# A graph network's second sum: rows sorted by source in three parts instead of one

## The reference

```
h = max(layernorm(x), 0)
msg = h[src] @ W_msg.T + b_msg + edge_embed[type]
x = x + gru(segment_sum(msg, dst), h)
h = max(layernorm(x), 0)
agg = segment_sum(h[dst], src)
z = ((1 + eps) * h + agg) @ W1.T + b1
x = x + relu(batchnorm(z) * gamma + beta) @ W2.T + b2
```

## Time and profile before

| | us |
|---|---|
| median of 3 runs | 6133.05 |
| lowest and highest | 6127.13 and 6144.72 |
| the profiled execution | 6150.87 |
| its span, first to last instruction | 6148.8 |
| busy in the span: PE, PEld | 3286.6, 2671.0 |
| DVE, ACT, POOL | 2171.7, 2000.3, 3592.3 |
| mean granted TensorE clock | 0.642 |

### The profile page before, as it was taken

How to read it: one execution, slowest core, us unless ns; L and a number is a source line. 1 busy time by engine, 2 the same in 40 slices (tenths; PEclk the granted TensorE clock), 3 DMA queues, 4 the chain that set the end, 5 groups by cost and what they waited for, 6 DMA issues and landing times.

```text
span 6148.8 us, 85445 instructions
## 1 busy us (share of the span) xinstructions
PE 3286.6 (53%) x19136; PEld 2671.0 (43%) x19137; DVE 2171.7 (35%) x4141; ACT 2000.3 (33%) x4208; POOL 3592.3 (58%) x3971
## 2 busy tenths in 40 slices
PE   4555556666666666667733333333433333337776
PEld 4444445445544544546532333222323323237775
DVE  8444444444444444445600000000000000027774
ACT  5222222222222222223522222221222212238886
POOL 2555556566665665663266666666666666666651
PEclk8555556665666556658755555555555555569999
DMA  4222211111111111111222222222212222236664
GB/s 141 57 58 56 55 52 42 41 42 42 43 43 40 43 43 40 43 43 53 65 72 71 73 71 71 72 71 69 74 68 75 71 69 74 69 114 224 221 221 142
DMA packets 251756, 466.50 MB, mean 76 GB/s; under 512 B 66550, under 2 KB 169129, under 8 KB 237581
## 3 DMA queue, kind: packets, MB, share of 16 engines
q0 software_dynamic: 106944, 226.05, 12.4%
q1 hardware_dynamic: 144717, 239.48, 11.9%
HBM read 315.00 MB, written 150.28 MB: 76 GB/s over the span
## 4 chain that ended last, share of the span: by engine, by line
another core or an unknown queue 34%; issue 24%; PE 23%; ACT 7%; SPq 6%; DVE 3%; ACTq 1%; DMA 1%; POOL 1%; DVEq 0%; POOLq 0%
PE ps L1563 7%; PE ps L1535 6%; PE ps L1410 4%; PE ps L1424 3%; ACT sb_counts L702 2%; SPq L405 2%; ACT ps L709 2%; SPq L406 2%; SPq L407 1%; PE ps L1432 1%; ACT sb_ring L788 1%; ACTq L784 1%; SPq L416 1%; DVE sb_oh L1237 1%
## 5 line engine op out<-in xcount | busy, mean ns | idle before, releaser
L573 POOL DMA_INDIRECT sb_ring<-msg_table,sb_idxslot x1664 | 1581.1, 950 | 1098.0 <-SPq L418 619.5
L603 POOL DMA_INDIRECT rows_by_src<-sb_ring,sb_idxslot x1664 | 1617.0, 972 | 864.4 <-issue 503.3
L1535 PE MATMUL ps<-sb_H,sb_oh 128*128 x3520 | 865.5, 414 | 1540.9 <-issue 1130.9
L1535 PEld LDWEIGHTS ps<-sb_H,sb_oh 128*128 128x128 f32 x3520 | 724.8, 299 | 1681.7 <-issue 1678.7
L1410 PE MATMUL ps<-sb_ring,sb_oh 128*128 x3520 | 849.2, 415 | 328.6 <-SPq L414 172.7
L1237 DVE TENSOR_SCALAR sb_oh<-sb_oh,sb_cf 128x512 f32<-128x512 bf16 x440 | 206.4, 492 | 2188.2 <-remote 1425.1
L1410 PEld LDWEIGHTS ps<-sb_ring,sb_oh 128*128 128x128 f32 x3520 | 734.7, 305 | 398.9 <-issue 392.2
L702 ACT CAST sb_counts<-ps 54x512 bf16<-54x512 f32 x440 | 254.4, 578 | 1919.0 <-remote 1030.5
L788 ACT COPY sb_ring<-ps 128x512 f32<-128x512 f32 x416 | 242.1, 582 | 1791.8 <-remote 1290.9
L1123 DVE TENSOR_TENSOR sb_Y<-sb_Y,ps 128x512 f32 x440 | 300.6, 683 | 746.8 <-remote 485.9
L1563 PE MATMUL ps<-sb_oh,sb_H 128*128 128x128 f32 x3520 | 432.6, 281 | 163.0 <-issue 116.8
(11 more groups left out here) (216 smaller groups left out, 3571.6 us busy)
## 6 DMA issues: line engine op xcount, KB each, us to landing
sb_H<-rows_by_src SPq DMA_DIRECT2D x110, 1088.0 KB, 5.0
sb_oh<-step_targets SPq DMA_DIRECT2D x110, 512.0 KB
sb_ring<-msg_table,sb_idxslot POOLq DMA_INDIRECT x1664
rows_by_src<-sb_ring,sb_idxslot POOLq DMA_INDIRECT x1664
rows_by_src<-sb_cf SPq DMA_DIRECT2D x198, 68.0 KB
msg_table<-sb_oh SPq DMA_DIRECT2D x14, 448.0 KB, 3.2
sb_oh<-in_x SPq DMA_DIRECT2D x49, 128.0 KB, 2.1
x_after_layer<-sb_H SPq DMA_DIRECT2D x49, 128.0 KB, 1.9
```

The source lines that it names most:

```text
L573: pool.indirect_dma_start(out=ring[:, r * G + q, 0:F], out_offset=None, in_=table_d[:, :], in_offset=bass.IndirectOffsetOnAxis(ap=idxslot[ ...
L603: pool.indirect_dma_start(out=rows_d[:, :], out_offset=bass.IndirectOffsetOnAxis(ap=idxslot[:, h, g * G + q:g * G + q + 1], axis=0), in_=r ...
L1535: m = mm(picked_ps[:, ds(slot, P)], pick[g][:, q * P:(q + 1) * P], H[:, ds(off, P)], start=False, stop=True, skip_group_check=True)
```

## The change

The tiles are cut into three parts of 768, 512 and 384 tiles (PASSES). Within each part the edges are sorted by source on their own: each part has its own starts of the 98 blocks (base_s has three rows), its own pads after each block, and its own stretch of rows_by_src: 55, 39 and 31 chunks, 125 in all (ALLC) against 110. As soon as all scatters of a part have landed, its chunks are summed within the pick stage (overlapped_sum on PE, sum_keys and sum_add on DVE, srows_in on SP), with two chunks of rows in flight; PICK_PHASES says in which pairs: none up to pair 27, then four sum chunks in each of the pairs 28 to 40 and three in 41, none in 42 and 43, four in each of 44 to 52 and three in 53. That is 94 chunks (OV). The last 31 are summed afterwards as before, with their counts set on by OV.

In the overlapped sums DVE alone makes the one-hots of the keys (four steps at a time) and adds the banks. ACT zeroes nothing: PE writes zeros to columns 128 to 511 of the bank with one matmul, and the group's first matmul begins its 128 columns anew (start).

In layer 0 DVE adds up the four one-hots of a group into one (block_sums, blks), so that rank_before and rank_after are one matmul each and not four. Where a part begins, PE sets the rank bank to that part's base (fresh).

In the prologue the digit one-hots are made from the packed edges in the tiles' own order, read back from DRAM (digit_fields at the third norm turn), so that each part is counted for itself; two of the 13 pieces follow after the loop. Pads: two for each block of each part, 588 in all against 196, each with one register load instead of two, over the first 294 groups of layer 0; the unused ends of the three stretches are filled with four larger pad blocks at the start. The table of the sums' blocks (sum_blocks) is worked out in the tail of layer 0 and not at its start.

```diff
+PASSES = (768, 512, 384)
+USED = [n + BLOCKS for n in PASSES[:-1]] + [(PASSES[-1] * P - PADS) // P + BLOCKS]
+SCHUNKS = [-(-(n + BLOCKS) // CH) for n in PASSES]
+FIRST_C = [sum(SCHUNKS[:z]) for z in range(NPASS)]
+OV = FIRST_C[-1]
+FCH = SCHUNKS[-1]
+ALLC = OV + FCH
...
         def rank_before(slot):
-            for q in range(G):
-                m = nc.tensor.matmul(rank_ps, before_b[:, :], own_blocks(slot)[:, q, :], start=False, stop=True,
-                                     skip_group_check=True)
-            return m
+            return nc.tensor.matmul(rank_ps, before_b[:, :], blks[:, slot, :], start=False, stop=True, skip_group_check=True)
...
+        def pick_loop(engine, body):
+            for a, b, s0, n in PICK_PHASES:
+                def pair(j):
+                    for k in range(2):
+                        sums = [((j - a) * 4 + s0 + i, (s0 + i) % 2) for i in range(2 * k, min(2 * k + 2, n))] if n else []
+                        body(j, k, sums, s0 if j is a and k == 0 and s0 in FIRST_C else None)
...
+            def pad_tile(a, b):
+                t = sp.value_load(lastrow[:, a, ds(b, 1)], min_val=0, max_val=ROWS_D - CH * P + CH - 1)
+                sp.dma_start(rows_d[ds(t, P, CH), :], const("pad")).then_inc(S("pads_out"), 16)
...
-            with sp.Fori(1, BLOCKS // RGROUPS) as j:
+            with sp.Fori(1, padded // RGROUPS) as j:
                 for r in range(RGROUPS):
                     relay(j, r)
                     pad_tiles(j * RGROUPS + r)
...
+            def landed(z):
+                for r in range(RGROUPS):
+                    sp.wait_ge(S(f"ring_dma{r}"), GATHERED + TILES_BY[z] // (RGROUPS * G) * G * 16)
+
+            def feed(j, k, sums, first):
+                c = j * 2 + k
+                if first is not None:
+                    z = FIRST_C.index(first)
+                    landed(z)
+                    for s, h in ((first, first % 2), (first + 1, 1 - first % 2)):
+                        wait(sp, "sum_done", (s - 1) * GPC)
+                        srows_in(s, h)
+                if not (isinstance(c, int) and c + 2 >= CHUNKS):
+                    sp.wait_ge(S("pick_oh"), (c + 1) * GPC)
+                    loc_in(c + 2, k)
+                for s, h in sums:
...
+                        sp.wait_ge(S("sum_done"), (s + 1) * GPC)
+                        srows_in(s + 2, h)
...
+            def block_sums(n, slot):
+                dve.wait_ge(S("blk_made"), n + 1)
+                vs.tensor_reduce(blks[:, slot, :], own_blocks(slot).rearrange("p q b -> p b q"), axis=AX.X, op=ALU.add) \
+                    .then_inc(S("blk_ready"), 1)
...
                         dve.wait_ge(S("rank_read"), n + 1)
                         vs.tensor_reduce(posE[:, ds(n * G, G)], own_ranks, axis=AX.X, op=ALU.add)
+                        block_sums(n + 1, (g + 1) % G)
...
+            def sum_keys(s, k, g):
+                if g == 0:
+                    dve.wait_ge(S(f"rows_in{k}"), rows_turn(s, k))
+                wait(dve, "sum_done", (s - 1) * GPC + g + 1)
+                vs.tensor_tensor(skeys[g].rearrange("p (q e) -> p q e", e=P),
+                                 srows[k][:, g * G:(g + 1) * G, KEY:KEY + 1].to_broadcast([P, G, P]),
+                                 iota_f.unsqueeze(1).to_broadcast([P, G, P]), ALU.is_equal).then_inc(S("key_oh_v"), 1)
+
+            def sum_add(s, g, offs):
+                n = s * GPC + g
+                dve.wait_ge(S("sum_done"), n + 1)
+                wait(dve, "bank_free", n)
+                yb = Y[:, ds(offs[g], 512)]
+                vs.tensor_tensor(yb, yb, bank(GPC + g), ALU.add).then_inc(S("bank_free"), 1)
+
+            def picks_and_sums(j, k, sums, first):
+                offs = [group_offsets(s, sumrow, (regs, regs_o)[i]) for i, (s, h) in enumerate(sums)]
+                layer1_pick(j, k)
+                for i, (s, h) in enumerate(sums):
+                    for g in range(GPC):
+                        sum_keys(s, h, g)
+                        if i:
+                            sum_add(sums[0][0], g, offs[0])
+                for g in range(GPC if sums else 0):
+                    sum_add(sums[-1][0], g, offs[-1])
...
+            def overlapped_sum(s, h):
+                step_offsets(s, sumrow)
+                for g in range(GPC):
+                    pe.wait_ge(S("key_oh_v"), s * GPC + g + 1)
+                    wait(pe, "bank_free", (s - 1) * GPC + g + 1)
+                    mm(bank(GPC + g)[:, P:], zeros_b[:, 0:P], zeros_b[:, P:], start=True, stop=True)
+                    for q in range(G):
+                        o = bank(GPC + g)[:, 0:P] if q == 0 else ps[:, GPC + g, ds(rel(g, q), P)]
+                        m = mm(o, srows[h][:, g * G + q, 0:F], skeys[g][:, q * P:(q + 1) * P],
+                               start=q == 0, stop=True, skip_group_check=True)
+                    m.then_inc(S("sum_done"), 1)
+
+            def picks_and_sums(j, k, sums, first):
+                picks(j, k)
+                for s, h in sums:
+                    overlapped_sum(s, h)
```

More of the change, by code:

```diff
@@ L63 @@
 DROWS, DW = DCOLS * NHI, DCOLS * NLO
+DIG_AT = 3
 NG = 2
@@ L235, in build_gnn @@
         lastf = small(BLOCKS)
-        lasti = [small(BLOCKS, i32) for _ in range(2)]
         possl = small(G, i32)
@@ L481, in _ @@
             loc_in(1, 1)
-            with sp.Fori(1, PAIRS) as j:
-                for k in range(2):
-                    sp.wait_ge(S("pick_oh"), (j * 2 + k - 1) * GPC)
-                    loc_in(j * 2 + k, k)
+            def feed(j, k, sums, first):
[10 more added lines that the diff above has]
+                for s, h in sums:
+                    after = [FIRST_C[z + 1] for z in range(NPASS - 1) if isinstance(s, int) and s < FIRST_C[z + 1]]
+                    if not (isinstance(s, int) and s + 2 >= after[0]):
+                        sp.wait_ge(S("sum_done"), (s + 1) * GPC)
+                        srows_in(s + 2, h)
@@ L608, in scatter @@
                         place_idx(b + 1, 1 - h, posE)
-            pool.wait_ge(S("pads_out"), (2 * BLOCKS + 2) * 16)
+            pool.wait_ge(S("pads_out"), 16 * sum(SCHUNKS[z] - USED[z] // CH for z in range(NPASS)) + NPASS * BLOCKS * 32)
             pool.wait_ge(S("posE_ready"), 1)
@@ L1447, in layer0 @@
                             rank_after((g + 3) % G).then_inc(S("rank_counted"), 1)
+                        if fresh is not None and g == 0:
+                            mm(rank_ps, ident, base_s[:, fresh, :], start=True, stop=True)
                         pe.wait_ge(S("blk_ready"), n + 1)
@@ L1457, in _ @@
             pe.wait_ge(S("base_s"), 1)
[L1458 to L1463 removed]
+            for z in range(NPASS):
+                a, b = (TILES_BY[z] - PASSES[z]) // (2 * CH), TILES_BY[z] // (2 * CH)
+                layer0(a, 0, fresh=z)
+                layer0(a, 1)
+                with pe.Fori(a + 1, b) as j:
+                    for k in range(2):
+                        layer0(j, k)
             for c in range(TCHUNKS, CHUNKS):
@@ L1617, in shape_constants @@
     put("blk", np.arange(NBK))
-    put("step", np.arange(SB) * P + np.arange(P)[:, None])
+    steps = np.arange(SS) * P + np.arange(P)[:, None]
+    put("step", steps)
+    put("done", -(BLOCKS - 1.0) * sum((steps >= FIRST_C[z] * CH) for z in range(1, NPASS)))
     put("lneps", LN_EPS)
```

335 lines of the change are left out of this document (199 added, 136 removed).

## The result

| | before | after |
|---|---|---|
| median | 6131.48 us (6127.13 to 6144.72, 4 runs) | 6309.15 us (6304.75 to 6318.91, 4 runs) |
| the profiled execution, its span | 6150.87, 6148.8 | 6312.55, 6310.1 |
| mean granted TensorE clock | 0.642 | 0.626 |

The ratio is 1.0297, 95% interval 1.0284 to 1.0309: the change makes this kernel 2.9% slower. That is the side and the mechanism forecast (6250, range 5790 to 6500), 59 us short. All of it is one trade: 395 us of sums taken from the end, 540 us given for them in the pick stage.

What follows compares the result with a forecast made beforehand. It took the crawl during POOL's unbroken DMA issue to limit the pick stage. Terms -395 + 499 + 10 + 0 - 6 + 10 + 7 = +125 on the 6148.8 span gave 6274, less 17.8: 6256, said as 6250 us, range 5790 to 6500.

Steps and rivals of the forecast that it cites:

- sum stage: Sums after the picks: 31 chunks left of 110, so 79 fewer at 5.0 us each, -395 us.
- 48 heavy turns: Pick stage: turns with sum chunks under the picks take 32.5 us against 22.1, +499 us.
- phase starts: Pick stage: at two starts SP waits for the part and loads two chunks, some 5 us each, +10 us.
- ranks: Layer 0: fewer rank matmuls on PE, a new reduction on DVE, neither on the path; 0, ends -120 and +120.
- pads: Layer 0: 294 padded groups instead of 98, one register load per pad, 6.5 us a group; -6 us.
- prologue: Start: digit fields moved to the third norm turn, larger pad blocks written; +10 us (0 to +25).
- tail, table of the sums: Sums' block table leaves layer 0's start (-3) and comes three times in the tail (+10): +7 us.
- crawl: Pick stage: every sequencer slows from 10 us into POOL's unbroken issue to 4.3 us after it, 13.5 us a heavy turn.
- rival (d): Layer 0: SP stays the chain for 294 padded groups, +165 us on the forecast, 6415 us; chance 0.08.
- Rival (a): Pick stage: POOL stays the bound, heavy turn 23 us, total -331, 5800 us, faster; chance 0.25.
- (b): Pick stage: half of the crawl, heavy turn 27.5 us, total -115, 6015 us; chance 0.15.
- (c): Pick stage: DVE's new one-hots lock POOL out, or PE stays at 1.2 GHz; turn about 37.4 us, 6490 us; chance 0.17.

Runs made afterwards that it cites:

- e4: The changed kernel with four rank matmuls before and four after per group again, without DVE's summed one-hots: 6342.02 us, ratio 1.0345 to the kernel before.
- e3: The changed kernel with three of each group's four scatters left out and pads over all 125 chunks: heavy turn 19.4 us, light turn 9.1 us.
- e2: The changed kernel with POOL zero fills (3.3 us) after every 8 scatters from scatter group 192 on: 5994.49 us, ratio 0.979.
- e10: The changed kernel with 3.3 us rests of POOL after every 16 scatters, on a crawling chip: 6015.92 us, ratio 0.982.
- e9: The changed kernel with one 1.7 us zero fill by POOL after every 8 scatters, on a crawling chip: 5868.41 us, ratio 0.958.
- e6: The changed kernel with one 1.7 us zero fill by POOL after every 8 scatters, on a chip that doesn't crawl: 5123.12 us, ratio 0.966.
- e7: The changed kernel with 3.3 us rests of POOL after every 16 scatters, on a chip that doesn't crawl: 5119.23 us, ratio 0.965.
- e1: The changed kernel with all 125 sum chunks after the picks and none under them: 6226.81 us, ratio 1.017 to the kernel before.
- e8: The changed kernel unaltered, run once more on a crawling chip: 6298.16 us, ratio 1.027 to the kernel before.
- e11: The changed kernel with 1.7 us rests after every 8 scatters plus 0.8 us fills before every second gather group in layer 0: 5884.84 us, ratio 0.959.
- e5: The kernel before with a pad's two register loads made one, on a chip that doesn't crawl: 5250.62 us, ratio 0.991.
- e12: The kernel before with 1.7 us rests of POOL after every 8 scatters, on a chip that doesn't crawl: 5456.88 us, ratio 1.030.

## Why the prediction was right

Measured terms, from the starts and ends of the stages in both traces; the sum is 6310.1 - 6148.8 = +161.

| term | said | measured |
|---|---|---|
| sum stage | -395 | -395 (560.4 to 165.4) |
| 48 heavy turns | +499 | +515 in 46 of them |
| phase starts | +10 | +72 in the other 2 |
| light turns around them | 0 | -47 |
| ranks | 0 | -24 (up to -40, see e4) |
| pads | -6 | +19 (the gathers' -5 less the ranks) |
| prologue | +10 | +20 |
| tail, table of the sums | +7 | +1 |

- The sum stage: 79 fewer chunks at 5.0 us, exact.
- The heavy turn: forecast 32.5 us, measured 33.5 without the two phase starts (22.3 before in the same places). The mechanism was right, but that the size is so near is in part luck, since two errors cancel. PE's work is less than I said (19.4 us a turn in e3, with POOL's part small, for 21.2). The crawl's length nearly holds (from the first update at 9.9 us into the burst to the flush 2.3 us after POOL's last scatter 12.8 us, for 13.5), though its start doesn't: the update that comes out at 9.9 us belongs to a matmul that ended at 4.1, so updates were held by then. And what comes after it is longer than said: I had let the picks begin at once, and they stand behind DVE's additions and 2.5 us of its register loads. I named that queue and gave it no price.
- The phase starts were mis-sized. I priced the loading of rows (some 5 us) and not the state of the ring. The first heavy turn takes 55.0 us. PE comes to its sums with the ring full, POOL has rows for 32 scatters on end (to 4318.1), and the sums fall into a crawl of 30 us. Here even the first sum chunk crawls, within a group, where nothing has to be waited for: one matmul in 1.4 to 3.5 us, put down to issue, where eight take 1.05 us at other times. The last line is DVE, which waits for it:

```profile
4299.33 0.37 PE L1706 MATMUL ps<-sb_ranked,sb_stepE 128*128 128x128 f32 x1 [1.74 <-issue]
4301.44 0.37 PE L1706 MATMUL ps<-sb_ranked,sb_stepE 128*128 128x128 f32 x1 [1.74 <-issue]
4303.53 0.37 PE L1706 MATMUL ps<-sb_ranked,sb_stepE 128*128 128x128 f32 x1 [1.72 <-issue]
4307.03 0.37 PE L1706 MATMUL ps<-sb_ranked,sb_stepE 128*128 128x128 f32 x1 [3.12 <-issue]
...
4324.00 0.69 DVE L1367 TENSOR_TENSOR sb_stepE<-sb_stepE,sb_cf 128x512 f32<-128x512 f32 x1 [37.50 <-remote]
```

- Light turns give 47 us back: after the heavy ones PE is no longer waiting for ring slots, and the picks between and behind the phases run ahead (turns of 9 to 23 us).
- Layer 0: the reduction of block_sums reads its bf16 input with a stride and takes 811 ns, not the 558 I took from the fp32 one beside it. It gained 24 us even so. Padded groups take 6.5 us as said (370 gathers in 600 us, 6.49 us a group), and rival (d), with 7.1, is out. But groups without pads take 6.19 and not 6.25, so the 294 padded ones cost 88 us against them, where before's 98 cost 79. The +19 of the table is only what is left of the stage without the ranks, and as uncertain as they are.
- The prologue: the read-back of the packed edges from DRAM, which I had hidden behind the norm turns, is waited for.

```profile
DVE sb_Y L1099 <- DMA sb_Y<-packed_edges: 18.0, 1, 18.0
```

- The 59 us from 6250 to 6309: 36 are the terms above (161 for 125). 14 come from taking 17.8 us off for the difference between before's profiled run and its median, where the profiled run of after lies only 3.4 above its own. 6 are the rounding of 6256, the rest the difference between a span and its run.
- Rival (a), POOL stays the bound, is what happens on the chips that don't crawl (turn 24.0 with rests, with POOL hardly waiting for rows under the sums). (b)'s 27.5 us a turn lie between e2 and e10. (c) had two halves. PE's clock: I said over 0.8 in heavy turns, and it is 0.68 on the whole. The first sum chunk runs at the higher level (1.05 us for eight matmuls), the second, after 4 us of standing, at the lower one (1.8 to 1.9 us). In e3, where the chunks follow each other, it is 0.88. The lock-out exists, and is small in the change. Of the 1664 scatters of the change (and of e9), by what DVE did meanwhile:

| DVE meanwhile | scatters, mean us: change | e9 |
|---|---|---|
| nothing | 1300, 0.966 | 989, 0.967 |
| additions (one PSUM input) | 40, 0.967 | 203, 0.967 |
| new one-hots (two SBUF inputs) | 65, 1.021 | 84, 1.373 |
| both | 79, 1.113 | 126, 1.042 |
| one-hots of the picks | 179, 0.994 | 234, 1.004 |
| new one-hots and those of the picks | 1, 0.967 | 26, 1.533 |

That is 15 us of POOL's time in the change, against the 68 that I had allowed. But only 115 of the 376 new one-hots there meet a scatter at all, since POOL mostly stands when DVE makes them. In e6, where it doesn't, 362 do, and they cost 89 us, 1.8 us a heavy turn, which accounts for e6's turn of 24.0 where I had expected 22.5. The Trainium skill, "SBUF — State Buffer" (SBUF: two separate sides), says which operations take the port, those with two inputs in SBUF among them, and the table agrees: additions with an input in PSUM delay nothing, one-hots with two inputs in SBUF do, a single scatter up to 3.62 us in e9. Its "whole instruction" is not the usual price, though; most of the scatters that overlap a new one-hot lose under 0.1 us (147 of 236 in e9). Sometimes it is more than one instruction: all 109 scatters of over 2 us in e2, e6, e7 and e9 begin beside the four new one-hots that DVE makes back to back, and end 0.84 us after the last of them.

## What to carry to other kernels

Before work is moved into the idle time of an engine, look at what that idle time is made of. Here it was time in which handshakes didn't get through. Only the first sum chunk, which has no handshake within it and lies early in the burst, fitted into it for nothing; late in a long burst it crawled as well. A bound engine that never pauses can be a cost to the others: 1.7 us of useless work after every 8 DMAs turned a change of +2.7% into one of -4.2%. Count queued work at the start of a phase too: a full ring makes the first turn the worst.

## What the runs showed of the hardware

- The kernel before took a median of 6128 to 6131 us in three sets of runs and 5299 in two others, on other chips, each set within 0.4% of its median. (e1 to e4 and e8 to e11 ran on two chips of the first kind, e5 to e7 and e12 on two of the second.) The difference goes with the crawl: on the second kind register instructions stay at 68 to 74 ns through 2100 us of unbroken DMA issue by POOL, on the first they take up to 1410 ns (median still 74). A scatter and its issue take the same on both. No chip was seen in both ways, so whether this belongs to the chip or to its state at that time isn't known. A prediction from one profile holds for that kind of chip.
- What is held back on the first kind is semaphore updates above all: in the cycle shown one of PE's in 6.4 us while POOL issues, then 0.1 us apart once it stops, the oldest 15.5 us late. In the long burst of the first heavy turn PE's own instructions come late too, a matmul in 1.4 to 3.5 us. When it begins isn't one number: in the burst above the update of a matmul that ends 4.1 us into it is late already (POOL had stood for 13 us before), in e9's the one after 8.0 us is in time. What sets the start stays open; "some 10 us" fits the register instructions and the time of the first late update. I had read a general slowness of the sequencers from the earlier trace rows. The register instructions of the sums don't show it, with 159 ns each even in that long burst; what grows there is the time between instructions. Why either is held isn't shown. The trace loses records on this kind, too: of ACT's 415 copies into the ring 246 have their update on record in the kernel before, all 415 in e5; whether the recording has a part in the crawl, no run here tells.
- A rest needn't be idle: zero fills by POOL itself let the others through just as a wait does. 1.7 us after every 8 DMAs are enough most of the time.
